# Seven groups of node tiles: 4, 4, 4, 4, 4, 3, 2 in place of 4, 4, 4, 4, 3, 3, 3

## What is computed

```python
node_feats = layernorm(x)
for _ in range(6):
    h = maximum(node_feats @ W1.T + b1, 0) @ W2.T + b2
    msg = segment_sum(h[src], dst, num_segments=n_nodes)
    gx = msg @ W_ih.T + b_ih
    gh = node_feats @ W_hh.T + b_hh
    r = sigmoid(xr + hr); z = sigmoid(xz + hz)
    n = tanh(xn + r * hn)
    node_feats = (1 - z) * n + z * node_feats
x = x + node_feats
# router: top 2 of 8 by layernorm(x) @ Wg + bg + bias, softmax over the two
# out = sum over the two of w * (relu(x @ F1[e] + fb1[e]) @ F2[e] + fb2[e])
x = x + out
```

## Time and profile before

| | us |
|---|---|
| median of 3 runs | 1929.82 (1929.55 to 1931.87) |
| profiled execution | 1928.45 |
| its span, first to last instruction | 1926.6 |
| TensorE matmul busy | 1813.1 |
| VectorE busy | 1082.1 |
| ScalarE busy | 622.2 |

### The profile page before, as it was taken

The page is one execution under the profiler, slowest core; times in us unless marked ns, Lnnn a source line. Parts: engine busy times, 40 slices in busy tenths (PEclk is TensorE's granted clock), DMA queues, the critical chain, the costliest instruction groups (busy, mean ns, idle before and its releaser), DMA issues.

```text
span 1926.6 us, 30095 instructions
## 1 busy us (share of the span) xinstructions
PE 1813.1 (94%) x10713; PEld 1089.6 (57%) x10714; DVE 1082.1 (56%) x2575; ACT 622.2 (32%) x1285; POOL 331.6 (17%) x443
## 2 busy tenths in 40 slices
PE   4799999999999999999999999999999999839996
PEld 3554555556445664456644566445674556539996
DVE  7888888854445643445434454334553466636775
ACT  2544444434121241222411224121241112216664
POOL 2011111101555400000000000000000032234565
PEclk8899999999999999999999999999999999959999
DMA  8950000002343300000000000000000011654543
GB/s 257 335 181 1 2 1 2 2 1 87 128 142 130 108 2 1 1 1 1 2 1 1 1 1 2 1 1 1 1 1 1 12 54 46 250 225 76 88 74 55
DMA packets 74245, 109.61 MB, mean 57 GB/s; under 512 B 12077, under 2 KB 65112, under 8 KB 72818
## 3 DMA queue, kind: packets, MB, share of 16 engines
q1 hardware_dynamic: 49724, 49.17, 8.1%
q0 software_dynamic: 18368, 38.09, 8.0%
q10 hardware_dynamic: 6006, 20.40, 2.7%
HBM read 43.59 MB, written 65.05 MB: 56 GB/s over the span
## 4 chain that ended last, share of the span: by engine, by line
PE 72%; issue 14%; POOL 7%; DVE 4%; ACT 1%; DMA 1%; POOLq 0%; ACTq 0%; DVEq 0%
PE bank L1663 36%; PE bank L1687 25%; PE bank L1638 5%; PE bank L1713 5%; POOL out L643 3%; POOL slot_in L620 2%; POOL tick L642 1%; DMA out<-slot_y,dest 1%; ACT stage L1365 1%; DVE hot_key L894 1%; DVE st L701 0%; POOL rstd L612 0%; DMA e_dst<-in_dst 0%; DVE hot_row L888 0%; DVE x_lo L754 0%
## 5 line engine op out<-in xcount | busy, mean ns | idle before, releaser
L1663 PE MATMUL bank<-adj,r_hi 128*128 128x512 fp8e4 (+4 forms) x2100 | 730.1, 352 | 0.0
L1663 PE MATMUL bank<-adj,r_lo 128*128 128x512 fp8e4 (+4 forms) x2016 | 702.2, 352 | 0.0
L1663 PEld LDWEIGHTS bank<-adj,r_hi 128*128 128x128 f16 x2100 | 205.6, 98 | 188.0 <-issue 0.8
L1663 PEld LDWEIGHTS bank<-adj,r_lo 128*128 128x128 f16 x2016 | 197.3, 98 | 179.3 <-issue 0.8
L781 DVE SCALAR_TENSOR_TENSOR m_lo<-bank,msg_unit,m_hi 128x512 f16<-128x512 f32 (+4 forms) x84 | 57.2, 682 | 284.7 <-ACT m_hi L1295 280.4
L1687 PE MATMUL bank<-x_hi,wht_hi 128*128 128x512 f16 (+4 forms) x504 | 177.3, 352 | 0.5 <-DVE m_lo L781 0.5
L1687 PE MATMUL bank<-m_hi,wct_hi 128*128 128x512 f16 (+4 forms) x504 | 177.3, 352 | 0.0
L1687 PE MATMUL bank<-m_hi,wct_lo 128*128 128x512 f16 (+4 forms) x504 | 177.3, 352 | 0.0
L1687 PE MATMUL bank<-m_lo,wct_hi 128*128 128x512 f16 (+4 forms) x504 | 177.3, 352 | 0.0
L1687 PE MATMUL bank<-x_hi,wht_lo 128*128 128x512 f16 (+4 forms) x504 | 177.3, 352 | 0.0
L1687 PE MATMUL bank<-x_lo,wht_hi 128*128 128x512 f16 (+4 forms) x504 | 177.3, 352 | 0.0
(11 more groups left out here) (309 smaller groups left out, 2804.5 us busy)
## 6 DMA issues: line engine op xcount, KB each, us to landing
slot_in<-fill_rows SPq DMA_DIRECT2D x2, 13520.0 KB, 65.2
ffn_scratch<-pair POOLq DMA_DIRECT2D x32, 512.0 KB, 3.3
ffn_w<-ffn_scratch ACTq DMA_DIRECT2D x8, 2048.0 KB, 15.9
x_rows<-in_L_ffn_W POOLq DMA_DIRECT2D x32, 256.0 KB, 3.9
slot_x<-slot_in SPq DMA_DIRECT2D x30, 260.0 KB, 3.1
xa<-in_x ACTq DMA_DIRECT2D x2, 1536.0 KB, 12.3
x<-in_x SPq DMA_DIRECT2D x1, 3072.0 KB
out<-x SPq DMA_DIRECT2D x4, 512.0 KB
```

Of the source, the lines that this page charges most:

```text
L1663: last = mm(bank[f][:, 0:n], r[:, q, f * P:(f + 1) * P], c, start=q == 0 and i == 0, stop=q == NT - 1 and i == len(todo) - 1)
```

## The change

One constant: the dealing of the 25 tiles to the groups.

```diff
-WIN_TILES = (4, 4, 4, 4, 3, 3, 3)
+WIN_TILES = (4, 4, 4, 4, 4, 3, 2)
```

## The result

| | before | after |
|---|---|---|
| median of the runs shown beside each other, us | 1930.84 (1929.55 to 1931.87) | 1955.93 (1952.21 to 1957.26) |
| ratio | 1 | 1.0128 [1.0113, 1.0143] |
| span of the profiled execution, us | 1926.6 | 1955.4 |
| granted TensorE clock, mean | 0.976 | 0.971 |

The change makes the kernel slower by 1.3%, some 25 us. The prediction was slower by 13 us, 1943, range 1935 to 1949: the direction was right, the size half of what came, and the time lies outside the range. Which terms failed is said behind the experiments.

A forecast was written before the change was run, and what follows sets the result against it. The prediction took TensorE, busy 94% of the span, as the bound, with VectorE and ScalarE working in its shadow. Two shadows of 3.1 us over four steps (+12.4) plus +0.5 in the last step gave 1943 us, range 1935 to 1949.

The forecast's parts named there:

- the last step's +0.5: Last step with the router between: later tail start and shorter tail and scatter nearly cancel, +0.5 us taken.
- TensorE's sum, 0: Steps 1 to 5: group 4's longer and group 6's shorter matmuls cancel, 9.1 us each way a step; 182 columns take 78.3 ns.
- rival A: Group 6's matmuls: weight loads bind, one 182-column matmul every 98 ns; +23 us, 1953; chance 0.11.
- the 25 ns: Group 6's matmuls: the skill page's surcharge per load and matmul pair, if it held at 182 columns; time near 1957.
- Shadow 1: Steps 1 to 4, before group 6's first gates: TensorE waits 1.5 us a step for VectorE's msg_lo of the last group.
- Shadow 2: Steps 1 to 4, before relu sums 2, 4, 6, 8: TensorE waits 0.4 us each for ScalarE's bank fill, 1.6 a step.
- rival B: Loop's return: the gap grows up to 1.3 us at each of three returns, +3.8 us, 1947; chance beyond the bounds 0.04.
- the start of the tail: Last step: VectorE's tail, which begins with msg_lo(6,1), starts 7.0 us later, up to 9.4.
- the shrinking of the tail: Last step: narrower group 6 work saves about 4.8 us and two fewer scatter transfers 2.5.
- What stays hidden: Step's end: relu_lo(9) ties with TensorE's last 24 gate matmuls, and the loop's gap covers it anyhow; no cost.
- Rival C: The shadows hold and rows(4) has no wait, so only the last step's -2.7 us is left, 1927; chance 0.10.
- D: Rival: only one of the two waits at the step's end is there, +6 to +8 us, 1937; chance 0.12.

The follow-up runs named there:

- e3: Kernel after, with five unused 512-column matmuls added at the end of each pass of TensorE's loop: ratio 1.0126 against the kernel before.
- e9: Kernel after, with TensorE's steps 1 to 4 written out without a loop, other engines unchanged: ratio 1.0055 against the kernel before.
- e14: Kernel after run again unchanged, on chip 3: ratio 1.0123 against the kernel before, last part 509.8 us.
- e6: New dealing in the last step and router alone, old dealing in the loop, on chip 5: ratio 1.0015 against the kernel before.
- e7: New dealing in steps 1 to 4 alone, old dealing in the last step: ratio 1.0085 against the kernel before.
- e10: Kernel before, with TensorE's steps 1 to 4 written out without a loop: ratio 0.9978 against the kernel before.
- e16: New dealing in the last step alone, old one in the loop, run a second time, on chip 3: ratio 1.0038 against the kernel before.
- e13: Kernel after, with four relu banks in place of two and TensorE's steps written out: ratio 1.0024 against the kernel before.
- e5: Kernel after, with the last group's msg_lo first and relu sums refilled over four banks in place of two: ratio 1.0059 against the kernel before.
- e15: Tiles dealt 4, 4, 4, 3, 4, 3, 3 and TensorE's steps written out: ratio 0.9971 against the kernel before.

## Why the prediction was right in direction and half in size

What failed is the last step's +0.5, for which 9.5 us came, and with it the way back and TensorE's clock, both put at no cost, for which 2.9 and 3.4 us came. The two shadows, nearly the whole of the forecast, were right.

- **TensorE's sum, 0.** Right. The 182-column matmuls come 78.3 ns apart (24 in 1.88 us, 49 in 3.84), so rival A and its 98 ns are out. So is the 25 ns that the page "TensorE: Matmul & The Clock Gate" of the Trainium skill, section Back-to-back issue gap, would add; its 81 ns at 128 columns is more than the 78.3 ns that the trace has at 182.
- **Shadow 1, 1.5 us, and Shadow 2, 1.6 us a step.** Right, in place and size. The waits are 1.12 us for m_lo, 0.12 before relu sum 2 and 0.32 before relu sums 4, 6 and 8; from start to start, with the 0.16 us by which matmuls overlap in the profile, about 1.3 and 1.7 us, and 3.04 us together by step 4 of after. Four steps: 12.2 us where 12.4 were forecast. What was missed is that they are one chain: either can be bought only with the other, until the ring has more banks.
- **The way back.** Left out of the sum and given to rival B, at up to 1.3 us a return. It was there: 1.0 us each by the gaps (6.7 against 3.8 us), 3 us in all. The working of B was right and its weight was wrong: the sum took the gap as fixed, without a reason. It stood in the profile as "issue", and e3 and e9 show that it depends on what lies ahead of it.
- **A half clock behind the longer gaps.** In no case of the prediction. Without their gaps steps 2 and 3 of after are 245.74 and 245.77 us, and the same steps at full clock in e14 244.05 and 244.07: 1.7 us each, 3.4 us in all.
- **The last step, +0.5.** The term that failed most: +9.5 in the trace. Its own working is short by 2.4 us: where the clock stays full behind rows(4), the new dealing costs 2.9 us (e6 against e7). The waits at rows(4) and rows(5) are 2.17 and 2.29 us, against 2.4 forecast for the first; the second was not forecast, it was 1.49 in before and 0.5 in e7 and e10. Against e7, e9 begins columns(5) 5.6 us later (7.0 forecast for the start of the tail), GpSimd issues its last scatter at the same time within 0.2 us, so the shrinking of the tail is 5.8 us (7.3 forecast), and the first tile of the FFN comes 2.2 us later, because the scatters land later. The rest has no term in the prediction. The last part of after is 9.8 us longer than that of e6: after is 6.0 us behind e9 at rows(5), by the stops and the half clock that e16 has too, 10.7 us at logits(5), with the stop in columns(5), and 8.3 at the first tile of the FFN. Against it stand 3.1 us by which before was itself slower there than e7, 2.3 of them in the FFN, where it had a half clock that e7 and e10 lack.
- **What stays hidden.** Right in after, where the gap covers relu_lo(9). e13 shows the 0.4 us that lie under it.
- **The account.** Two shadows 12.2, gaps 2.9, half clock at heads 3.4, last part 9.5, start 0.7: 28.7 of the 28.8 us between the two profiled executions. The forecast had the first and a small piece of the fourth. Rival C, that the shadows hold, is out; D, one shadow only, too.
- **The range.** It held no case in which TensorE's own durations change because it pauses. Five forecast pauses a step and one of 2.4 us in the last step were counted at their length alone. Two times inside rival A are also too high by its own working, which takes cover back from both shadows: the 25 ns would give about 1955 in place of 1957, and the pace of 107 ns some 4 us above 1953 in place of 8. Neither bears on the forecast.

## What to carry to other kernels

Matmuls of a narrow last tile are cover: before making them shorter, add up what other engines must do behind them, as one chain through the shared banks and not wait by wait; giving e5's ring two more banks was worth 9 us in steps 1 to 4, where reordering gave nothing. Where TensorE gets its first pauses of two microseconds and more, allow for a lower clock behind each, as a case of its own in the range. Compare versions on one chip before reading a few microseconds out of them: the same kernel gave 1.0015 on one chip and 1.0038 on another, with intervals that hardly overlap. And the way back of a loop is a cost that grows when the last matmuls get shorter; writing the loop out on TensorE alone made the kernel before 0.2% faster (e10), the best of all versions along with e15.

## What the runs showed of the hardware that was not expected

- After a pause of 1.99 to 2.65 us at a loop's head TensorE's granted clock fell to 0.50 for some 3 us in 12 of 21 cases, and after 1.05 to 1.80 us in none of 21; equal pauses of one kernel went either way. Each such fall cost 1.7 us.
- The same kernel (e6, e16) took 1928.2 to 1932.5 us in 11 executions on one chip and 1934.9 to 1939.8 in 5 on another, at another time; in the trace of the second the expert weights came in later, and TensorE had stops and a half clock that the first lacks.
- The gap at a loop's return was 1.05 to 1.66 us behind 24 matmuls of 310 columns, 2.0 to 2.65 behind 24 of 182, 1.3 to 1.8 with five of 512 more, and none in written-out code.
- TensorE stood 4.3 to 6.1 us between two transposes with nothing to wait for, in seven traces, while the DMA engines moved about 400 GB/s (379 to 441 in after), always at the same instruction; and not where the code ahead of it was of another length, or (0.98 us) the loads came later.
